# Order of passes: first feed-forward of the first four tiles ahead of the second one of tile 0, and the second one of tile 2 a pass later than its attention output

## The reference

```python
def ffn(x, W1, W2, W3):                    # 512 -> 2048 -> 512
    hidden = silu(x @ W1.T) * (x @ W3.T)
    hidden = fwht(hidden)                  # Hadamard transform, scaled by 1/sqrt(2048)
    return hidden @ W2.T

def attn(x, wq, wk, wv, wo):               # 16 heads of 32 features
    q, k, v = rope(heads(x @ wq.T)), rope(heads(x @ wk.T)), heads(x @ wv.T)
    w = softmax(einsum('bshd,bstd->bsht', q, k) / sqrt(32))   # s is the token, h and t are heads
    return einsum('bsht,bstd->bshd', w, v).reshape(...) @ wo.T

x = x + 0.5 * ffn(layernorm(x))
x = x + attn(layernorm(x))
x = x + 0.5 * ffn(layernorm(x))
```

## Time and profile before

| | before |
|---|---|
| median of three runs | 2519.74 us (2517.53 to 2520.3) |
| the profiled execution's own time | 2519.57 us |
| its span, first to last instruction | 2517.8 us |
| PE busy | 2504.8 us, 99% of the span |
| DVE busy | 2027.5 us, 81% |
| ACT busy | 528.8 us, 21% |
| POOL busy | 63.6 us, 3% |
| mean granted TensorE clock | 0.999 of full speed |

### The profile page before, as it was taken

How to read it: one execution, slowest core, us unless ns; L and a number is a source line. 1 busy time by engine, 2 the same in 40 slices (tenths; PEclk the granted TensorE clock), 3 DMA queues, 4 the chain that set the end, 5 groups by cost and what they waited for, 6 DMA issues and landing times.

```text
span 2517.8 us, 30105 instructions
## 1 busy us (share of the span) xinstructions
PE 2504.8 (99%) x11223; PEld 2074.0 (82%) x11223; DVE 2027.5 (81%) x2588; ACT 528.8 (21%) x810; POOL 63.6 (3%) x111
## 2 busy tenths in 40 slices
PE   9999999999999999999999999999999999999999
PEld 7878888888888888888888888888888888888887
DVE  9558978799786997979969889697886988978711
ACT  3322221222121221122212222122221212211211
POOL 0030000000000000000000000000000000000000
PEclk9999999999999999999999999999999999999999
DMA  9644635256452454525625546354562545535364
GB/s 340 251 188 177 213 138 190 101 199 202 169 207 76 176 210 162 203 100 200 203 89 208 167 180 211 118 213 146 200 208 76 186 165 210 185 115 200 134 219 165
DMA packets 112404, 446.89 MB, mean 177 GB/s; under 512 B 11201, under 2 KB 36033, under 8 KB 79041
## 3 DMA queue, kind: packets, MB, share of 16 engines
q1 hardware_dynamic: 82080, 420.26, 45.8%
q10 hardware_dynamic: 30240, 25.57, 3.4%
HBM read 402.79 MB, written 33.55 MB: 173 GB/s over the span
## 4 chain that ended last, share of the span: by engine, by line
PE 95%; DVE 4%; DMA 1%; ACT 0%; issue 0%; SPq 0%; DVEq 0%; ACTq 0%
PE gu L583 21%; PE gu L584 21%; PE gu L585 21%; PE acc L615 8%; PE acc L614 8%; PE acc L618 8%; PE acc L583 2%; PE acc L585 2%; PE acc L584 2%; PE acc L644 1%; DMA prod<-up_raw 1%; PE acc L709 1%; DVE prod L1263 1%; DVE mixed L1272 0%; DVE x L1202 0%; DVE w_up L1323 0%
## 5 line engine op out<-in xcount | busy, mean ns | idle before, releaser
L583 PE MATMUL gu<-xt,w_up 128*128 128x512 f32 x2048 | 798.6, 390 | 0.6 <-DVE xt L1138 0.4
L585 PE MATMUL gu<-xt,w_up 128*128 128x512 f32 x2048 | 796.9, 389 | 0.0
L584 PE MATMUL gu<-xt,w_up 128*128 128x512 f32 x2048 | 796.7, 389 | 0.0
L583 PEld LDWEIGHTS gu<-xt,w_up 128*128 128x128 f32 x2048 | 384.5, 188 | 81.6 <-issue 1.5
L584 PEld LDWEIGHTS gu<-xt,w_up 128*128 128x128 f32 x2048 | 384.5, 188 | 79.7
L585 PEld LDWEIGHTS gu<-xt,w_up 128*128 128x128 f32 x2048 | 384.5, 188 | 79.6
L1031 ACT ACTIVATE gated<-gu 128x512 f32<-128x512 f32 x240 | 143.6, 599 | 1137.8 <-PE gu L585 1137.8
L1525 DVE TENSOR_TENSOR gated<-gated,gu 128x512 f32<-128x512 f32 x240 | 163.2, 680 | 271.8 <-ACT gated L1031 271.2
L614 PE MATMUL acc<-w_down,hid 128*128 128x512 f32 x896 | 349.4, 390 | 0.0
L615 PE MATMUL acc<-w_down,hid 128*128 128x512 f32 x896 | 348.6, 389 | 0.0
L1258 DVE TENSOR_TENSOR prod<-tok 128x1024 f32<-128x1024 f32 x256 | 309.0, 1219 | 0.9
(11 more groups left out here) (141 smaller groups left out, 1956.0 us busy)
## 6 DMA issues: line engine op xcount, KB each, us to landing
w_up<-up_pairs SPq DMA_DIRECT2D x240, 1024.0 KB, 4.8
w_down<-down_pairs SPq DMA_DIRECT2D x240, 512.0 KB, 3.4
up_pairs<-w_up SPq DMA_DIRECT2D x16, 1024.0 KB, 4.9
xt<-tok ACTq DMA_DIRECT2D x144, 64.0 KB, 4.1
prod<-up_raw SPq DMA_DIRECT2D x16, 512.0 KB, 6.1
down_pairs<-w_attn SPq DMA_DIRECT2D x4, 2048.0 KB, 18.1
out<-x ACTq DMA_DIRECT2D x7, 1024.0 KB, 5.9
x<-x ACTq DMA_DIRECT2D x6, 1024.0 KB, 7.3
```

The source lines that it names most:

```text
L583: nc.tensor.matmul(o, w_hi, m_hi, start=first, stop=False)
L584: nc.tensor.matmul(o, w_hi, m_lo, start=False, stop=False)
L585: return nc.tensor.matmul(o, w_lo, m_hi, start=False, stop=last)
```

## The change

Only the table `PASSES` is different. All else that moves follows from it through the functions named above.

```diff
-PASSES = ((1, 0), (1, 1), (1, 2), (2, 0), (1, 3), (2, 1), (1, 4), (2, 2),
-          (1, 5), (2, 3), (1, 6), (1, 7), (2, 4), (2, 5), (2, 6), (2, 7))
+PASSES = ((1, 0), (1, 1), (1, 2), (1, 3), (2, 0), (2, 1), (1, 4), (1, 5),
+          (2, 2), (2, 3), (1, 6), (1, 7), (2, 4), (2, 5), (2, 6), (2, 7))
```

## The result

| | before | after |
|---|---|---|
| median of 14 runs each | 2519.68 us (2517.53 to 2520.74) | 2515.14 us (2513.75 to 2517.02) |
| the profiled execution's own time | 2519.57 us | 2515.13 us |
| its span | 2517.8 us | 2513.3 us |

The ratio is 0.9984, with a 95% interval of 0.9977 to 0.9992: 4.0 us faster, between 2.0 and 5.8 (the two medians themselves differ by 4.5). The forecast was 2516.1.

The account below looks back on a forecast made before the run. PE, busy 2504.8 of 2517.8 us, bounds the kernel, so only fewer instructions or waits pay. Terms -3.72 + 1.2 + 0.2 - 1.10 = -3.4 us against 2519.57 give 2516.1 us, range 2513.8 to 2518.9.

Parts of the forecast that it names:

- Part 1: Gaps ahead of passes 3 and 7: late gaps become early, without 16 transposes each; 1.86 us gained in each, 3.72 in all.
- the pattern of 160.42: Distance between first matmuls of passes around an early gap with attention output and moved input, without a wait; forecast 160.46 us.
- Part 2, pass 2: End of pass 2: exponential, line 932 and table load delay SiLU of step 15; PE waits about 1.2 us.
- The slack of 0.55 us: End of pass 2: how late SiLU of step 15 may come before PE's last down waits; 0.55 us.
- Part 2, pass 6: Pass 6 takes on the next input's statistics, norm and transposes on DVE; a wait of 0.2 us.
- my two bounds: Wait of pass 6: next to none as in pass 5, or 1.04 us as in pass 9.
- Part 3: Pass 8 to 9: sub 20 is early, its four transposes leave the gap; gain 1.10 us.
- Part 4: Tiles 4, 5 and 6 are loaded in the pass that takes their statistics; costs nothing, 11.8 us to spare.
- The rival with a late load: Step 6: loads land after their statistics are due, DVE stops; 2524.6 us or more; 5 in 100, with other slowdowns.
- No new waits: Rival: passes 2 and 6 get by as pass 5 does; -4.8 us, 2514.8; 14 in 100.
- The waits eat the gain: Rival: pass 2 waits 2.5 us, pass 6 1.04, pass 8 0.5; -0.8 us, 2518.8; 13 in 100.
- The extra 1.4 us of drain at a table load: Pass 2: SiLU of step 15 starts 1.4 us after its table is in; wait 2.6, time 2517.5; 2 in 100.

Follow-up runs that it names:

- the exchange: Changed kernel with line 932 (high half of the moved input) ahead of the exponential on ScalarE in step 14, concerning pass 2 alone; 2514.87 us, ratio 0.9983.

## Why the prediction was right

- *Part 1, right.* Pass 6 to 7 gave 1.89 us (forecast 1.86), without any wait. The trace of before carried this number in two places, and both held when tried: taking the wait out of pass 9 gave the pattern of 160.42 (forecast 160.46), and doubling the block gave 1.75 for a block between transposes. One detail was told inexactly. I said that the block of 16 into `acc` is gone from two gaps. The block that is gone is that of the normalized tile; the block of the attention output is left, and that is the one written into `acc` now, at 476.19.
- *Part 2, pass 2, right in mechanism and size.* 9.89 us between the two SiLUs for 9.89, and a wait of 161.69 - 160.42 = 1.27 us for 1.2. What I didn't see is the layer below it: with ScalarE's delay gone, DVE is 0.43 us late. The slack of 0.55 us was that of ScalarE's chain, counted as if DVE stood ready at SiLU(15). It had no effect on the forecast, but an estimate of what the repair brings would have been 0.4 too high, and the expectation of the exchange was.
- *Part 2, pass 6, too high by 0.2.* Of my two bounds the one of pass 5, no wait, was the true one.
- *Part 3, right:* 1.10 us, from pass 8 to 9 147.77. 0.77 of it is the wait for the norm of sub 20, which the prediction took in with the rest.
- *Part 4, right, and its margin was understated.* The loads cost nothing. The rival with a late load was to decide from the point where statistics wait at all (landings of 20.2 us), and to bite from 23 us. The experiment with the later load let DVE wait 1.15 us in pass 5 and 2.92 in pass 10, with no trace on PE. In those two passes its price begins further out. Where wasn't measured, since by the code a still later load stands behind a wait of ScalarE that DVE releases only behind these statistics; and in pass 6 no load came late.
- *Rivals.* "No new waits" (2514.8) lies nearer to the median than the forecast does (2516.1), but it is not what happened: the wait of pass 2 is there, in full. "The waits eat the gain" fell with pass 6 and pass 8, which have none. The extra 1.4 us of drain at a table load that the Trainium skill gives ("ScalarE: Activation LUTs", What ACT_TABLE_LOAD costs) is not seen: the load at 463.78 lasts 1.28 us and SiLU starts at 465.07, 0.01 behind its end.
- *The sum.* -3.64 us in the passes for -3.4; the 0.24 between them are pass 6 and rounding. The other 0.8 us by which the profiled execution beat 2516.1 is no term of the change: it is a dip of the clock that this execution missed (-1.52) and a start that came 0.71 later. That my start value, the profiled execution of before, had such a dip in it I didn't see, though the row was in the trace; it cost nothing here, since its time lay at the median. What stays open is 0.3 to 0.5 us: executions of the same kind differ by 3.9 to 4.1 us between the kernels, the distances from pass 2 on by 3.64. The interval of the ratio (2.0 to 5.8 us) holds both, and the start of up(15) in pass 0 alone, same code in all, lies between 108.1 and 110.5 us in the fourteen profiles.

## What to carry to other kernels

Where one engine is busy for 99%, subtract distances between like rows of it (first matmul to first matmul): they repeat within 0.05 us where the whole varies by 3, so a change of 0.1% can be added up term by term, and what a wait is worth read off by comparing with the same pattern without it. Price the repair of a wait only after asking what is late next behind it: here an engine's order hid a second wait of 0.43 us, and making the awaited value one unit sooner cleared both, where reordering cleared one and made a new one elsewhere. Sooner is not the rule: in pass 9 one unit later cleared the wait. And look at the granted clock behind every idle stretch of TensorE: one of 2.5 us was followed by a loss of another 1.5 here in six executions of ten.

## What the runs showed of the hardware that I had not expected

A single wait of 2.54 us of TensorE, in a kernel that otherwise keeps it at 99%, was followed in some executions by 3.4 us at a granted clock of 0.5, and in others, after the same wait, by none: 109 of 182 unfilled executions show the lower mean clock. It cost 1.5 us in the profiles of before and after, which is more than half of the wait itself. With eleven small matmuls of zeros in front of the wait, 1.47 us long, none of 11 executions had it, and no distance grew by them.
